# Mixture-of-experts loop: expert numbers read into TensorE's registers eight at a time instead of one at a time

## The reference, cut to what matters

```python
logits = jnp.einsum('bsh,eh->bse', x, router_w) + expert_bias
scores = jax.nn.softmax(logits, axis=-1)
top_w, top_idx = jax.lax.top_k(scores, TOP_K)
top_w = top_w / jnp.sum(top_w, axis=-1, keepdims=True)
g = jnp.einsum('bsh,khe->bske', x, gate_proj)
u = jnp.einsum('bsh,khe->bske', x, up_proj)
act = jax.nn.silu(g) * u
out = jnp.einsum('bske,keh->bskh', act, down_proj)
sel = jnp.take_along_axis(out, top_idx[..., None], axis=2)
return jnp.sum(sel * top_w[..., None], axis=2)
```

## Time and profile before

| | us |
|---|---|
| median of 3 runs | 1603.51 (1603.0 to 1612.21) |
| span of the profiled execution | 1595.4 |
| around the span (median less span) | 8.1 |
| expert loop, from the first gather (546.1) to the last scatter (790.1) in that execution | 244 |

### The profile page before, as it was taken

How to read it: one execution, slowest core, us unless ns; L and a number is a source line. 1 busy time by engine, 2 the same in 40 slices (tenths; PEclk the granted TensorE clock), 3 DMA queues, 4 the chain that set the end, 5 groups by cost and what they waited for, 6 DMA issues and landing times. The chain is left out here.

```text
span 1595.4 us, 26869 instructions
## 1 busy us (share of the span) xinstructions
PE 1121.8 (70%) x7861; PEld 525.6 (33%) x7861; DVE 1184.0 (74%) x3595; ACT 927.9 (58%) x1839; POOL 458.3 (29%) x608
## 2 busy tenths in 40 slices
PE   2555655655542488788627588999898999677996
PEld 1112212222121255555415233233333333243554
DVE  4799999999975743333376569999999999477664
ACT  2698889889864232332236246666666666546453
POOL 0212232231310666666411002222222222212331
PEclk9655555555555599999959789999999999978998
DMA  1246656557452512122172411111111111130001
GB/s 59 85 108 132 124 111 136 109 124 137 91 91 93 142 62 69 62 66 68 57 231 84 153 65 61 61 54 57 58 54 61 60 58 51 44 69 1 1 14 41
DMA packets 224864, 127.69 MB, mean 80 GB/s; under 512 B 168448, under 2 KB 204416, under 8 KB 224464
## 3 DMA queue, kind: packets, MB, share of 16 engines
q1 hardware_dynamic: 204672, 100.12, 25.2%
q0 software_dynamic: 6320, 15.54, 3.0%
q10 hardware_dynamic: 13728, 10.30, 2.5%
HBM read 54.33 MB, written 37.62 MB: 58 GB/s over the span
## 5 line engine op out<-in xcount | busy, mean ns | idle before, releaser
L1811 ACT ACTIVATE qkv_made<-qkv_lower 128x1024 f32<-128x1024 f32 (+3 forms) x256 | 208.0, 872 | 94.1 <-PE qkv_lower L1628 94.1
L1974 DVE CUSTOM_DVE_ANT_0 all_y<-qkv_upper,all_mask 128x384 bf16<-128x384 f32 (+3 forms) x512 | 231.5, 485 | 17.2 <-PE qkv_upper L1592 11.1
L1592 PE MATMUL qkv_upper<-l_k,all_y 64*128 64x512 bf16 (+3 forms) x768 | 208.5, 334 | 48.3 <-DVE qkv_mx L1978 25.6
L1857 POOL TENSOR_SCALAR_AFFINE_SELECT qkv_made<-qkv_made 128x256 f32<-128x256 f32 x256 | 102.5, 406 | 408.9 <-ACT qkv_made L1811 318.9
L569 ACT ACTIVATE a_rows<-a_rows 128x128 bf16<-128x128 bf16 (+7 forms) x256 | 173.1, 676 | 60.8 <-DVE a_rows L676 56.7
L666 DVE CUSTOM_DVE_ANT_0 a_rows<-a_sc,all_mask 128x128 bf16<-128x128 f32 (+7 forms) x256 | 192.1, 750 | 19.4 <-PE a_sc L520 18.4
L520 PE MATMUL a_sc<-a_k,a_q 16*128 16x512 bf16 (+3 forms) x384 | 167.2, 504 | 51.1 <-DVE a_mx L666 43.8
L1978 DVE TENSOR_REDUCE qkv_mx<-qkv_upper 128x1 f32<-128x512 f32 x256 | 173.0, 686 | 7.5 <-PE qkv_upper L1592 7.3
L1628 PE MATMUL qkv_lower<-all_y,l_k 64*128 64x384 bf16 (+3 forms) x768 | 173.4, 330 | 7.0 <-DVE all_y L1995 1.2
L1647 PE MATMUL qkv_upper<-qkv_made,qkv_v_heads 128*32 128x384 f32 (+3 forms) x1920 | 177.8, 434 | 0.0
L578 ACT ACTIVATE a_unread<-a_rows 128x128 bf16<-128x128 bf16 (+7 forms) x256 | 170.6, 666 | 0.0
(11 more groups left out here) (255 smaller groups left out, 1933.0 us busy)
## 6 DMA issues: line engine op xcount, KB each, us to landing
qkv_made<-out_rows SPq DMA_DIRECT2D x16, 512.0 KB, 8.0
l_k<-k_rows SPq DMA_DIRECT2D x64, 128.0 KB
o_rows<-qkv_made SPq DMA_DIRECT2D x32, 256.0 KB, 2.0
all_y<-q_rows SPq DMA_DIRECT2D x128, 48.0 KB
a_turned_sb<-a_rows SPq DMA_TRANSPOSE x256, 2.6
a_raw<-in_gate ACTq DMA_DIRECT2D x16, 224.0 KB, 3.3
a_raw<-in_up ACTq DMA_DIRECT2D x16, 224.0 KB, 4.2
ride_wd<-in_down SPq DMA_DIRECT2D x1, 3584.0 KB, 17.0
```

Of the source, the lines that this page charges most:

```text
L1592: nc.tensor.matmul(row[:, n % SLOTS, 0:w], q_sb[of_head, u % RING, POS[qb] * P:(POS[qb] + 1) * P], k_sb[of_head, u % RING, lo:lo + w], sta ...
L1811: nc.scalar.activation(probs[:, n % GR, lo:hi], st[:, n % 2, lo:hi], ACT.Exp).then_inc(exp_done, 1)
L1974: nc.vector.tensor_tensor_reduce(out=passed[:, n % SLOTS, 0:w], in0=tile[:, 0:w], in1=mask[:, at:at + w], scale=1.0, scalar=-3e38, op0=ALU ...
```

## The change

The constant `READ = 8` is new. In PE's loop the expert numbers are no longer read one per step. At every eighth step (i = 0, 8, ..., 72) one instruction reads eight integers of `which` (seven at i = 72) into as many registers, and each of them gets its own check. The other steps read nothing. What `gate_up` and `down` do with the registers is as before, as are all other engines' programs.

```diff
+READ = 8
...
             pe.wait_ge(which_ready, 1)
             for i in range(TILES + 3):
                 if i < TILES:
-                    expert[i] = pe.value_load(which[0:1, i:i + 1], min_val=0, max_val=E - 1)
+                    if i % READ == 0:
+                        read = range(i, min(i + READ, TILES))
+                        _, values = nc.values_load_multi_w_load_instructions(which[0:1, i:read.stop], engines=[mybir.EngineType.PE],
+                                                                             min_val=0, max_val=E - 1)
+                        expert.update(zip(read, values))
                     turn_in(i)
```

## The result

| | kernel before | kernel after |
|---|---|---|
| median of the runs | 1603.53 us (1603.0 to 1612.21, 4 runs) | 1618.8 us (1613.17 to 1624.65, 4 runs) |
| ratio after / before | | 1.0094, 95% interval 1.0064 to 1.0123 |
| span of the profiled execution | 1595.4 us | 1617.1 us |
| loop, from the first gather to the last copy of a result | 546.1 to 789.4, 243.3 us | 548.6 to 810.2, 261.5 us |

The account below looks back on a forecast made before the run. It took POOL and PE, waiting for each other in holds, to bound the loop. 200 us would become 175 to 176, gaining 24, less 4.5 of remaining holds: 19.5; span 1575.9 plus 8.1 gives 1584.0 us, range 1570 to 1613.

Parts of the forecast that it names:

- What bounds the loop: Loop: POOL could run at 2.57 us a tile, PE at 2.37; it runs at 3.08, POOL's waits for ACT total 39.1 us.
- Part (2): Loop: if single reads cause the holds, most go; at most 32.4 us gained, less 4.5 us for holds that remain.
- the early hold without a slow read: Early in the loop ACT waits 2.21 us until 575.41 although nearby reads took 297 and 301 ns; counted against reads as cause.
- no holds without gathers: End of the loop: after the last gather at 772.8 reads and scatters go on, PE busy 12.42 of 14 us.
- Rival A: Loop: POOL's back-to-back gathers and scatters cause the holds, which stay; pause mostly hidden, 0 to 6 us, 1604 to 1610; chance 0.27.
- Part (1): PE's sequencer: 69 of 79 reads go; direct gain 0 to 0.18 us a tile, taken as 0.
- Part (3): PE's sequencer: eight checks come in one piece; seven more at 0.27 us each, 1.9 us (1.2 to 2.9).
- Part (4): PE's sequencer: reading eight values takes 0 to 2.1 us more than reading one, taken as 0.7 us more.
- The pause: PE at every eighth tile: stands still 2.6 us (1.2 to 5.0) for the wide read and checks outlasting the down passes.
- rival B: Loop: holds stay and the pause outlasts a slack of 2.2 us; slower, taken at 1620 us; chance 0.14.
- Part (5): PE's clock in the loop: no fall taken; a tile at half clock per pause would cost some 2 us, 20 in all.
- The sum's last term: Outside the profiled span: 8.1 us added to the forecast span of 1575.9 to give 1584.0 us.

Follow-up runs that it names:

- e4: Kernel before, but SP stores each tile's result by plain DMA in tile order in place of POOL's scatters (result not the layer's): 1548.59 us, ratio 0.9655.
- e1: Kernel before without reads or checks, each tile's expert a constant of the program: 1601.29 us, ratio 0.9991.
- e5: e4 plus a second indirect gather per tile on POOL, into a spare buffer nobody reads: 1598.44 us, ratio 0.9983.
- e6: e4 plus a memset of a spare tile on POOL after each gather: 1548.79 us, ratio 0.9677.
- e2: Kernel after, with its wide reads but without the register checks: 1607.18 us, ratio 1.0007.
- e12: e8 without the register checks: 1549.18 us, ratio 0.9652.
- e8: e4 with the change, eight-wide reads and checks included: 1567.01 us, ratio 0.9791.
- e7: Kernel after with READ = 4, reads of four values with four checks each: 1603.43 us, ratio 1.0031.
- e3: Kernel before, one read a tile, without the check: 1606.44 us, ratio 1.0014.
- e10: Kernel before plus a memset of a spare tile on POOL after each scatter: 1607.15 us, ratio 1.0025.
- e13: e4 with the next stage fetching its rows by 64 POOL gathers, whole result computed: 1615.56 us, ratio 1.0102 to the kernel before.

## Why the prediction was wrong

**What bounds the loop** (POOL's floor of 2.57 us, PE's 2.37, and holds of 39 us between): right. e4's PE pace of 2.32 confirms the second figure.

**Part (2), the failed step.** The gain of 32.4 - 4.5 us rested on "The slow ones are those that begin together with a gather ... both stand just ahead of a hold". e1 has no reads and keeps the holds (36.5 of 39.1 us), and in after, with 7 of 8 reads gone, they take 47.7 us; e4, e5 and e6 tie them to the second indirect DMA of a tile. What was against it stood in the text: the early hold without a slow read the earlier trace rows, and "no holds without gathers", which fits what e4 and e5 show of indirect DMAs. The slow read at the start of a gather is not the cause of the hold. Rival A named the cause rightly, at 0.27, though not the outcome: it had the pause mostly hidden.

**Part (1), the direct gain:** taken at 0; e1, without any read, gains 0.1% (0.2% at most by its interval). Right.

**Part (3), the checks:** taken at 0.27 us each, measured 0.28. Right.

**Part (4), the wide read:** taken at 0.7 us more, measured 594 - 307 = 287 ns more; four values take 333, so the steps are not equal. It lies under the down passes and costs nothing that shows (e2, e12). The Trainium skill's figure ("Runtime: NRT & Kernel Launch", section "Instruction fetch mechanics") of some 200 ns per register, which is for loads from HBM and gave an estimated 1.6 us, is not what this read from SBUF takes.

**The pause:** taken at 2.6 us (1.2 to 5.0), measured 0.5 to 2.1 on PE, 1.5 in the mean of seven (10.4 us), and 1.5 in e8. Too long by a good third, in the main because the wide read took 0.3 us more and not 0.7, and because part of the piece can lie under more than the down passes. A shorter pause alone would have made the forecast faster still, so the miss does not come from it.

**Where the pause goes: the second failed step.** Rival A held that of a pause of 2.6 us "most of it is hidden", 0 to 6 us in all, and rival B asked for a pause of 4.0 us. The pause was shorter than taken, and yet after is 15 us slower (10 to 20 by the interval), near the 18 us that the pieces cost where nothing can hide them (e8 less e4). e2 shows that the checks are what costs it. The slack of about 2 us was read in a cycle with a hold; but only one tile in three has one, the piece falls on every eighth whatever the phase, and in the other tiles PE and POOL are within 0.2 us of each other. That last is my reading; what the runs show is that pauses of 0.7 us at most (e7) still cost some 5 us. So rival B's outcome came about, but not by its sum: with a slack of 2.2 us a pause of at most 2.07 us would have cost nothing. That 1618.8 stands by its 1620 is luck.

**Part (5), the clock:** "I take no fall" was wrong; what hangs on it stays open. After's granted clock, 574 to 774 and around the piece at 624:

```profile
574.00:774.00 200.00, 167.51 (x864) 106.32 (x863) 66.97 (x180) 59.19 (x182) 119.39 (x122) 0.92 0.19 61
```

```profile
620.00:625.00 5.00, 3.66 (x18) 2.39 (x18) 1.78 (x6) 1.81 (x6) 2.43 (x4) 1.00 0.14 45
625.00:627.20 2.20, 0.14 (x2) 0.04 (x2) 0.45 (x2) 0.37 (x1) 1.90 (x2) 1.00 0.28 89
627.20:629.00 1.80, 1.80 (x7) 0.80 (x8) 0.00 (x0) 0.37 (x1) 1.19 (x3) 0.57 0.19 46
629.00:631.00 2.00, 2.00 (x8) 1.46 (x7) 0.69 (x2) 0.36 (x1) 0.83 (x1) 0.53 0.33 98
631.00:633.00 2.00, 2.00 (x14) 1.34 (x13) 0.43 (x2) 0.85 (x3) 0.81 (x1) 1.00 0.00 0
```

After the pause of 2.06 us PE runs at its lower level, 1.2 GHz, until 631: six gate_up matmuls in 2.42 us for 1.30. The length of the pause does not settle it: of the eight pieces in the stretch five have a slow gate_up (2.16 to 2.42 us) right behind them, two of these after pauses of 1.16 and 1.18 us, while behind the pause of 1.33 us it takes 1.30 us. Nor does a fall need a piece: between 574 and 774 e1, which has no pieces, shows five gate_up groups of 1.7 to 2.5 us, and e3 seven of 1.6 to 2.4. The mean over the stretch falls from 1.00 to 0.92. Is it the clock, then, that makes after slow? The same stretch of e1, and of e3:

```profile
574.00:774.00 200.00, 170.34 (x914) 109.83 (x913) 73.48 (x195) 64.56 (x196) 127.05 (x130) 0.95 0.20 65
```

```profile
574.00:774.00 200.00, 169.63 (x901) 111.25 (x899) 72.34 (x194) 60.85 (x192) 125.27 (x129) 0.94 0.20 64
```

They have 0.95 and 0.94 and 6 us more of busy PE than before, and their times are before's; e10 has 0.93 at a ratio of 1.0025. So a mean of 0.93 to 0.95 goes with times close to that of the kernel before, whose profiled execution was a quick one at 1.00. And e8's 18 us come at a clock of 1.00. The pauses alone could thus make up the 15 us, if the loop with holds hides little of them; but among the 24 runs of the kernel before on e1's chip, too, the longer ones tend to have the lower mean clock (1599.38 us at 0.801, 1613.01 at 0.795), and no run separates the two in after. How much of the 15 us is the clock stays open.

**The sum's last term:** "8.1 around it" was the distance from a quick execution to the median. Nothing of the miss hangs on it.

## What to carry to other kernels

What runs beside a wait in a loop that repeats itself will always run beside it: before a gain is built on such a pair of rows, look for one case of the wait without the partner. Gathering small sequencer work into one instruction moves the rest of it (here the checks) into one piece too; ask what the piece lies under, and count the whole of what sticks out, since slack read in the best cycle isn't there in the others. Two indirect DMAs per step on one engine can slow a matmul loop by a fifth while no engine is busy all the time: a plain DMA for one of them took 42 us from this loop of 243, though it put the rows elsewhere, and fetching them from there cost more than that (e13).

## What was not expected of the hardware

- With two indirect DMAs of POOL per tile, 0.30 us apart, ACT's start on finished PE results comes 2 to 4 us late at about every third tile (17 times in 48 tiles before, 19 in 47 of e5). One per tile doesn't do it (1548.6 us), two do (1598.4), one with a memset of 0.54 us beside it doesn't (1548.8). What exactly starts a hold stays open.
- A load of PE's sequencer registers from SBUF takes 307 ns for one value, 333 for four and 594 for eight (medians).
- Eight checks of PE's sequencer take 2.2 us, and at 624 seven of them stick out from under the 1.12 us of down passes.
- TensorE's clock fell to its lower level behind pauses of 1.16, 1.18 and 2.06 us and not behind one of 1.33 us, and in e1 it fell without any such piece. What decides it stays open.
